# A three-stage block kernel: opening loads and weight split rearranged, pad rows written expert by expert

## The reference

```
mod = silu(c) @ wmod                     # six rows of 128 for each sequence
h = layernorm(x) * (1 + ca) + sa
x = x + ga * mamba(h)                    # 4-tap conv, selective scan with 16 states, gating
h = layernorm(x) * (1 + cb) + sb
x = x + gb * moe(h)                      # shared SwiGLU (938 wide) + top 2 of 8 SwiGLU experts
```

## Time and profile before

| what | us |
|---|---|
| median of 3 runs | 829.33 (828.41 to 831.73) |
| profiled execution | 833.42 |
| its span, first to last instruction | 831.6 |
| TensorE busy in the span | 690.9 (83%) |
| VectorE busy | 572.3 (69%) |
| ScalarE busy | 424.7 (51%) |
| GpSimd busy | 381.5 (46%) |

### The profile page before, as it was taken

One profiled execution on the slowest core, in us unless ns is written; L12 is line 12 of the kernel. 1 busy time (PEld: TensorE's weight loads), 2 busy tenths in 40 slices (PEclk: granted clock), 3 DMA queues, 4 the chain that ended last, 5 costly groups with the idle time before them and its releaser, 6 DMA issues.

```text
span 831.6 us, 11904 instructions
## 1 busy us (share of the span) xinstructions
PE 690.9 (83%) x3134; PEld 529.0 (64%) x3135; DVE 572.3 (69%) x1227; ACT 424.7 (51%) x821; POOL 381.5 (46%) x300
## 2 busy tenths in 40 slices
PE   3736889988888899887877998999989999999920
PEld 1425666756666676665645877777778777887710
DVE  3666888878788888888553665566656665666637
ACT  2413757475574757464433555555555555555510
POOL 2462264554446374555232745547228145632236
PEclk9758899999899999999787999999999999999975
DMA  7302000000000001000041203030303003000036
GB/s 236 88 1 70 20 27 25 26 25 19 6 32 19 25 26 25 26 25 27 7 162 62 95 24 108 12 108 24 98 23 94 26 16 108 25 25 27 28 108 205
DMA packets 38202, 44.37 MB, mean 53 GB/s; under 512 B 5334, under 2 KB 28880, under 8 KB 38184
## 3 DMA queue, kind: packets, MB, share of 16 engines
q1 hardware_dynamic: 33576, 35.69, 13.9%
q0 software_dynamic: 4608, 8.47, 3.1%
HBM read 31.42 MB, written 13.76 MB: 54 GB/s over the span
## 4 chain that ended last, share of the span: by engine, by line
PE 58%; DVE 22%; issue 8%; ACT 4%; DMA 2%; SPq 2%; POOL 2%; another core or an unknown queue 1%; DVEq 1%; ACTq 0%; POOLq 0%
PE PS L576 54%; PE PS L579 4%; DVE prod L1189 2%; DVE acc L1207 2%; DVE diag L1284 1%; DVE delta L1228 1%; DVE wd L1280 1%; DVE X L1308 1%; ACT L1021 1%; DVE r L1346 1%; DVE oh L1349 1%; DVE al L1194 1%; DVE stats_a L1174 1%; DVE r L1347 1%
## 5 line engine op out<-in xcount | busy, mean ns | idle before, releaser
L916 ACT ACTIVATE sg<-PS 128x512 f32<-128x512 f32 x216 | 129.3, 598 | 208.3 <-PE PS L576 179.0
L576 PE MATMUL PS<-xh,w_lo 128*128 128x512 f32 x432 | 188.6, 437 | 21.7 <-DVE prod L1189 10.5
L1189 DVE TENSOR_TENSOR PS<-PS,sg 128x512 f32<-128x512 f32 x160 | 111.9, 699 | 131.0 <-PE PS L576 111.1
L576 PE MATMUL PS<-xh,w_hi 128*128 128x512 f32 x432 | 172.8, 400 | 0.0
L576 PE MATMUL PS<-xl,w_hi 128*128 128x512 f32 x432 | 172.8, 400 | 0.0
L535 POOL DMA_INDIRECT result_dram<-y_rows,aux_d x80 | 78.0, 975 | 200.6 <-DVE y_rows L1540 161.8
L576 PEld LDWEIGHTS PS<-xh,w_lo 128*128 128x128 f32 x432 | 83.8, 194 | 52.5 <-issue 18.3
L469 POOL DMA_INDIRECT sorted_dram<-h,slot x64 | 71.3, 1115 | 93.3 <-DVE slot L1384 66.3
L1194 DVE TENSOR_TENSOR al<-PS,ah 128x512 fp32r<-128x512 f32 x160 | 109.2, 683 | 6.4 <-ACT ah L923 3.9
L923 ACT CAST ah<-PS 128x512 fp32r<-128x512 f32 x160 | 93.2, 582 | 15.2 <-DVE PS L1189 13.5
L576 PE MATMUL PS<-ah,w_lo 128*128 128x512 f32 x216 | 93.7, 434 | 4.0 <-ACT ah L923 4.0
(11 more groups left out here) (218 smaller groups left out, 1136.1 us busy)
## 6 DMA issues: line engine op xcount, KB each, us to landing
stage<-in_w_gu SPq DMA_DIRECT2D x18, 469.0 KB
xin<-sorted_dram SPq DMA_DIRECT2D x20, 260.0 KB, 2.6
stage<-in_w_dn SPq DMA_DIRECT2D x9, 448.0 KB
tab<-mods_dram SPq DMA_DIRECT2D x8, 384.0 KB, 3.5
sorted_dram<-pad SPq DMA_DIRECT2D x8, 260.0 KB
out<-X SPq DMA_DIRECT2D x4, 512.0 KB, 3.2
stage<-result_dram SPq DMA_DIRECT2D x3, 512.0 KB, 5.1
result_dram<-y_rows,aux_d POOLq DMA_INDIRECT x80
```

Of the source, the lines that this page charges most:

```text
L576: return nc.tensor.matmul(out, lhsT, rhs, start=start, stop=stop, **k)
L916: A.activation(sg[:, c % 3, :], bank("gate", where, c), ACT.Silu).then_inc(s["silu_done"], 1)
L1189: V.tensor_tensor(product_in(where, c), bank("up", where, c), sg[:, c % 3, :], ALU.mult).then_inc(s["prod_done"], 1)
```

## The change

Seven things change.

1. The three constants needed first (`mats`, `w_in`, `cols`) count on a semaphore `first_in` of their own, and only six on `consts_in`. SP no longer waits for the first chunks before it issues the next loads. `head_norm(0)` waits for no constants, `modulate(0)` only for the two modulation columns (`mods_cols`), and `project_in` no longer for `mods_rows`.
2. GpSimd clears only the three pad regions of `stage`, at the very start.
3. `head_moments` and `head_root` cover 4, 14 and 14 chunks instead of 4, 4 and 24. VectorE does the first 14 after `conv`, the other 14 after `make_delta`; GpSimd does the third root after `pairs_by_b(0)`.
4. The shared weights are split by ACT (one copy of 128x3072 to `w_hi`, after `keep_next` in `body(0)`) and VectorE (three subtractions of 128x1024, in `body(0)`).
5. GpSimd releases `split_done` 2 before `body(G-1)`, and SP loads the raw weights of x = 2 before it waits for the plan.
6. SP writes the pads of expert 0 only ahead of the first tile, and those of expert e+1 after the tile loads of expert e; the wait for `split_done` and the next raw load follow, and `tiles_of` stands behind these.
7. In the last shared expert the count matmul comes after chunk 2's gate and up, ACT does chunk c+1's silu ahead of chunk c's high part, VectorE one product ahead.

```diff
@@ sync
-            load_x(0, GC)
-            sp.wait_ge(s["x_in"], 16)
+            load_x(0, GC, "x_in")
...
-            const(mats[:].rearrange("p m t -> p (m t)"), a["big"])
+            first(mats[:].rearrange("p m t -> p (m t)"), a["big"])
...
-            load_x(GC, CH - GC)
+            load_x(GC, CH - GC, "x_more")
...
+            sp.wait_ge(s["split_done"], 2)
+            load_raw(2)
             sp.wait_ge(s["plan_ready"], 1)
             sp.wait_ge(s["setup_mem"], 2)
-            for e in range(E):
-                row = sp.value_load(plan[0:1, 2, e:e + 1], min_val=e * REGION, max_val=e * REGION + TOKENS)
-                sp.dma_start(sorted_dram[bass.ds(row, TILE)].rearrange("(p r) d -> p (r d)", p=P),
-                             pad[:].rearrange("p r d -> p (r d)")).then_inc(s["pads_out"], 16)
-            sp.wait_ge(s["pads_out"], 16 * E)
+            pad_rows(0)
             sp.wait_ge(s["sorted_out"], 16 * 2 * CH)
...
-            with sp.Fori(0, E - 1) as e:
-                expert(e, True)
-            count = expert(E - 1, False)
+            with sp.Fori(0, E - 2) as e:
+                expert(e)
+                pad_rows(e + 1)
+                sp.wait_ge(s["split_done"], e + 3)
+                load_raw(e + 3)
+            expert(E - 2)
+            pad_rows(E - 1)
+            count = expert(E - 1)
@@ gpsimd
-            pool.wait_ge(s["mods_pe"], 1)
-            V.memset(stage[:], 0.0).then_inc(s["stage_clear"], 1)
             pool.wait_ge(s["consts_in"], 16 * NCONST)
-            head_root(2, GC, GC)
             expand_c(0)
-            split_hi(0, 0)
-            head_root(3, 2 * GC, CH - 2 * GC)
+            head_root(2, GC, EARLY)
@@ tensor
-                    count_picks(G - 1, LAST_COUNTS)
                 if c == 2:
                     pe.wait_ge(s["y_out"], G - 1)
                 if c < FC:
                     gate_up(0, G - 1, c, WIDE)
+                if c == 2:
+                    count_picks(G - 1, LAST_COUNTS)
@@ scalar
+            def split_high():
+
+                act.wait_ge(s["raw_in"], 16 * NRAW)
+                A.copy(w_hi[0][:], stage[:]).then_inc(s["split_hi"], 1)
...
-            act.wait_ge(s["consts_in"], 16 * NCONST)
             head_norm(0, 1)
-            act.wait_ge(s["mods_rows"], 1)
+            act.wait_ge(s["mods_cols"], 1)
             modulate(0)
+            act.wait_ge(s["first_in"], 16 * NFIRST)
@@ vector
+            dve.wait_ge(s["x_more"], 16)
+            head_moments(GC, EARLY)
             dve.wait_ge(s["a_neg_ready"], 1)
...
             make_delta(0)
+            head_moments(GC + EARLY, CH - GC - EARLY)
             level_exponents(0)
...
             pairs_by_c(0)
-            head_moments(2 * GC, CH - 2 * GC)
```

More of the change, by code:

```diff
@@ L298, in _, with load_x, first @@
             x_view = a["x"].rearrange("(c p) d -> p c d", p=P)
[L300 to L301 removed]
+            def load_x(c0, n, done):
+                sp.dma_start(X[:, c0:c0 + n, :], x_view[:, c0:c0 + n, :]).then_inc(s[done], 16)
             def const(dst, src):
                 sp.dma_start(dst, src).then_inc(s["consts_in"], 16)
[L306 to L307 removed]
+            def first(dst, src):
+                sp.dma_start(dst, src).then_inc(s["first_in"], 16)
+            load_x(0, GC, "x_in")
             sp.dma_start(c_t[:], a["c_t"]).then_inc(s["c_in"], 16)
             sp.dma_start(stage[:, 0:6 * P], a["L0_wmod"]).then_inc(s["c_in"], 16)
[L310 to L312 removed]
+            first(mats[:].rearrange("p m t -> p (m t)"), a["big"])
+            first(w_in[:].rearrange("p m t -> p (m t)"), a["L0_attn_W_in"])
+            first(cols[:], a["cols"].rearrange("(h p) d -> p h d", p=P))
+            const(w_x[:], a["L0_attn_W_x"].rearrange("(h p) d -> p h d", p=P))
+            const(a_log[:], a["a_log"].to_broadcast([P, NS]))
             const(small[:], a["small"])
@@ L344, in _, with pad_rows @@
                 load_tab_g(g)
+            def pad_rows(e):
+                row = sp.value_load(plan[0:1, 2, bass.ds(e, 1)], min_val=0, max_val=(E - 1) * REGION + TOKENS)
+                sp.dma_start(sorted_dram[bass.ds(row, TILE)].rearrange("(p r) d -> p (r d)", p=P),
+                             pad[:].rearrange("p r d -> p (r d)")).then_inc(s["pads_out"], 16)
+            sp.wait_ge(s["split_done"], 2)
+            load_raw(2)
             sp.wait_ge(s["plan_ready"], 1)
             sp.wait_ge(s["setup_mem"], 2)
-            for e in range(E):
-                row = sp.value_load(plan[0:1, 2, e:e + 1], min_val=e * REGION, max_val=e * REGION + TOKENS)
-                sp.dma_start(sorted_dram[bass.ds(row, TILE)].rearrange("(p r) d -> p (r d)", p=P),
-                             pad[:].rearrange("p r d -> p (r d)")).then_inc(s["pads_out"], 16)
-            sp.wait_ge(s["pads_out"], 16 * E)
+            pad_rows(0)
             sp.wait_ge(s["sorted_out"], 16 * 2 * CH)
@@ L360, in load_tile, with expert @@
                     s["tile_in"], 16)
-            def expert(e, more):
+            def expert(e):
                 tiles, first = tiles_of(sp, e)
-                if more:
-                    sp.wait_ge(s["split_done"], e + 2)
-                    load_raw(e + 2)
+                sp.wait_ge(s["pads_out"], 16 * (e + 1))
+                apart(sp)
                 with sp.Fori(0, tiles) as t:
@@ L1044, in _ @@
             pair_decays(0)
-            def step(I, c, where):
-                silu(I, c, where)
-                high(I, c, where)
             def body(g, prev, head):
@@ L1064, in body @@
                 keep_next(g)
+                if not prev:
+                    split_high()
                 if prev:
@@ L1111, in _ @@
             copy_h2(G - 1)
+            silu(G - 1, 0, WIDE)
             for c in range(FC):
-                if c == 1:
+                if c + 1 < FC:
+                    silu(G - 1, c + 1, WIDE)
+                if c == 0:
                     router_exp(G - 1)
-                step(G - 1, c, WIDE)
+                high(G - 1, c, WIDE)
             keep_result(G - 1, WIDE)
@@ L1323, in second_norm, with split_low @@
                 V.engine_nop().then_inc(s["tab_free"], 1)
+            def split_low(k):
+                n = WC // 3
+                at = slice(k * n, (k + 1) * n)
+                if k == 0:
+                    dve.wait_ge(s["split_hi"], 1)
+                last = V.tensor_tensor(w_lo[0][:, at], stage[:, at], w_hi[0][:, at].bitcast(F32), ALU.subtract)
+                if k == 2:
+                    last.then_inc(s["split_done"], 1)
             def low_x(g):
@@ L1458, in body @@
                 gate_y(g, 0)
+                if not prev:
+                    split_low(0)
                 if prev:
@@ L1463, in body @@
                 gate_y(g, 1)
+                if not prev:
+                    split_low(1)
                 if prev:
@@ L1469, in body @@
                 tail_moments(g)
+                if not prev:
+                    split_low(2)
                 if prev:
@@ L1507, in _ @@
             product(g, 0, WIDE)
+            weights(g)
             low(g, 0, WIDE)
-            weights(g)
             place(g, LAST_COUNTS)
@@ L1522, in _ @@
             V.engine_nop().then_inc(s["aux_read"], 1)
+            product(g, 1, WIDE)
             for c in range(1, FC):
-                product(g, c, WIDE)
+                if c + 1 < FC:
+                    product(g, c + 1, WIDE)
                 low(g, c, WIDE)
```

33 lines of the change are left out of this document (16 added, 17 removed).

## The result

| kernel | median, us | ratio to the kernel before, 95% interval |
|---|---|---|
| before | 830.28 (828.41 to 831.73) | |
| changed | 810.09 (808.52 to 812.65) | 0.9767 (0.9734 to 0.9800) |
| changed, second comparison | 808.06, beside 829.66 | 0.9744 (0.9710 to 0.9779) |
| changed, third comparison | 808.38, beside 830.95 | 0.9757 (0.9721 to 0.9793) |

The change is worth 20.2, 21.6 and 22.6 us in the three comparisons, 21.5 on average. The profiled execution of the changed kernel took 809.22, span 807.4; that of the kernel before had taken 833.42. The pair differs by 24.2. The prediction had 24.5 for the pair and 804.8 for the median; the measured median is 810.1, inside its range of 798 to 813, with a gain 3 us smaller than forecast.

The account below looks back on a forecast made before the run. TensorE is busy 83% of the span; the prediction took its waits in the opening and at the hand-over as the losses addressed. 16.3 + 8.2 = 24.5 us off 829.3 gives 804.8, range 798 to 813.

Parts of the forecast that it names:

- First projection 4.9 ahead: Opening: modulation inputs 2 us sooner, head norm waiting for the shift alone; projection starts at 11.4, 4.9 us ahead.
- Scan factors 6.0 ahead: End of `pairs_by_c`: 4.9 + 0.8 - 1.4 - 1.3 + 3.0 from `take_dbc`, `delta`, moments' overrun and `lev_c`.
- Mixing 20.3 ahead: Opening: TensorE's matrices become the last input, 7.1 us behind `pairs_by_c`; `mix` starts at 44.5 instead of 64.81.
- 3.1 lost to ACT's copy: First gating product: ACT's 2.7 us copy delays `conv(1)`, so 6.8 us from the matrices instead of 3.7.
- 0.9 lost to the third subtraction: Between `tail_moments` and `take_dbc`: VectorE's subtraction puts softplus ahead of ACT's tail norm; 0.9 us lost (0 to 2.5).
- Loop entered 16.3 ahead: Start of the looped groups: 20.3 - 3.1 - 0.9 = 16.3 us ahead.
- Looped groups 0: Looped groups wait only on the program's own progress, so an earlier start should reach the end whole.
- Hand-over 8.2: First tile: gated result at 432.2 and tile landing at 432.3 meet; start near 432.5, 8.2 us ahead (6 to 9).
- Borders 0, tiles 0: Expert borders: tiles issued 1.2 to 1.6 us later, but slack of 0.6 or more; 0 lost (to 4).
- From the profiled execution to the median: Whole kernel: profiled execution would come to 808.9; the median, 4.1 lower, loses the same 24.5 us, to 804.8.
- first two rivals: First: split stays on the path, 812, chance 0.13. Second: expert borders starve, four at 1 to 2 us, 810, chance 0.10.
- third rival: More than forecast: `delta` is not blocked, or TensorE's clock is higher in the denser opening; 798, chance 0.09.

Follow-up runs that it names:

- e1: The changed kernel timed once more with no edit, beside the kernel before at 829.66: 808.06 us, ratio 0.9744.

## Why the prediction was right, and where its terms were off

The median of 810.1 (808.1 and 808.4 later) lies in the range of 798 to 813, and the mechanism is the forecast one. The gain itself was forecast 3 us too large, and the small gap of the profiled pair (24.2 against 24.5) is luck, as the terms show:

- **First projection 4.9 ahead.** 16.34 - 11.62 = 4.7. The inputs of the modulation came only 1.0 sooner (6.22), not 2.0; in e1 they came at 5.49 and the projection started at 11.12, 5.2 ahead. Items 1 and 2 were not run alone, so this term rests on these rows.
- **Scan factors 6.0 ahead.** GpSimd's pairs and VectorE's end as forecast: `pairs_by_c` ended at 36.4 (it started at 35.14, 1.28 long), where it had started at 41.39, so 6.3. All four pieces are in the rows: no late `take_dbc`, `delta` 1.41, the moments' overrun, `lev_c` 0.42.
- **Mixing 20.3 ahead.** It was 22.8 (64.81 - 42.04), or 21.8 over four profiles with the old opening (mean 63.94) and four with the new (42.11). The forecast took TensorE's 7.1 us from `pairs_by_c` to its matrices as a constant. They were measured at a granted clock of 0.50 (42.60 to 49.65); here it was 0.70 from 36.4 to 40 and 1.00 from 40 to 48, and TensorE needed less. The run with the moved subtractions had the same program up to mixing and a clock of 0.50 from 35.7 to 43: 43.45 - 35.13 = 8.3 from GpSimd's pairs to mixing, against 42.04 - 35.90 = 6.1.
- **3.1 lost to ACT's copy.** 22.8 ahead at mixing, 20.1 at the first gating product (67.78 - 47.70): 2.7. The copy was forecast at 2.7 and took 2.76.
- **Not forecast: 1.7 lost to the half clock.** VectorE's gating, with a subtraction between the two halves, left TensorE idle for 5.19 us, and the output products took 3.75 instead of 2.02.
- **0.9 lost to the third subtraction.** From 18.6 ahead at the end of the output products (76.19 - 57.55) to 17.8 when group 1's pairs start on GpSimd. The row `rstd_b` shows why: 1.03 us beside the subtraction, 0.24 in the run where the subtraction stood elsewhere. This is the blocking the other way round, of GpSimd by a VectorE operation, which the rows of before had not shown. By the rule on the shared ports (the Trainium skill, SBUF — State Buffer, "SBUF: two separate sides") it should happen, and the trace agrees.
- **Loop entered 16.3 ahead.** It was 17.8 to 18.9, by which engine one takes. Over four profiles with the old opening (mean 89.44) and four with the new (71.63) it is 17.8 by TensorE's first shared product, and 16.9 by GpSimd's pairs of group 1 (89.16 and 72.29). The 0.9 between the two is the router's products ahead of the loop, which took 2.2 to 2.4 us in the four old profiles and 1.66 in the new ones, as the granted clock was higher there (0.70 from 88 to 90.3 in the kernel before, 1.00 from 70 to 74 in the changed one).
- **Looped groups 0.** From the first shared product to the last `tab_g` it is 315.05 us on average in the four old ones and 316.65 in the four new. So 1.6 were given back by that mark, and 0.7 from GpSimd's pairs on: more than half of the 1.6 is the head start of TensorE alone that was just named. Two of the new ones are at 315.3 and two at 318.0, one of each on the same chip, so four profiles can hardly tell the rest from nothing; what sets a group's pace there stays open.
- **Hand-over 8.2.** The pair shows 8.2 (34.70 - 26.47 from the last `tab_g` to the first tile), but by chance, and twice. Over three profiles with the old SP order the 34.70 is 33.98, and over the nine with both items and the new order the 26.47 is 28.3. So the term is 5.7 (6.6 for the three profiles of the changed kernel alone). The step that failed is "the last down products lose waits of 2.2 and 0.4 us ... the gated result comes at 432.2 instead of 436.2": of these 4.0 us the order gives next to nothing (no gain in time alone, at most half a microsecond in the profiles), and the pause of 1.91 at 428.05, which I let it absorb, stands in no other profile.
- **Borders 0, tiles 0.** 0.17 at one border; from the first tile to the results 362.5 before, 363.1 and 361.9 and 361.8 after.
- **From the profiled execution to the median.** The prediction took the same 24.5 off the median, as if the two executions differed by a constant 4.1. But the profiled execution of before was long in just the places above: by 0.9 in its opening, 0.6 in its groups and 0.7 in its hand-over against the means just given. Part of what I counted as gain was that. The sum that the marks give is 17.8 - 1.6 + 5.7 = 21.9, and the measured one 21.5.

By the time alone the first two rivals (812 and 810) fit the 810.1 better than the 804.8; it is the rows that rule their mechanisms out. The split did not stay on the path as in the first one: ACT's copy took 2.76 and not 5.3, and `diag` 0.69. Part of its conditions held, though: a low clock behind the opening, and a blocked operation at the third subtraction. The borders did not starve. Of the third rival one condition held, the higher clock ahead of mixing, and it was worth some 2 us there (6.1 against 8.3); the half clock at the output products took 1.7 back.

## What to carry to other kernels

A queue's order counts by what stands between the last event and the transfer that is waited for: moving four issues out of there gave nearly all of the hand-over's gain, while seven pads less gave next to nothing. Before an operation is moved to another engine, list which operations of the neighbour it will run beside, and not only those that were slow before; a wait taken from one pair can come back at the next. And a profiled pair that agrees to 0.3 us with the forecast proves little when single executions of one kernel differ by 4: set each term against several profiles, and by the marks of more than one engine. A clock that comes back in one stretch can be lost in the next: look at the granted clock up to the mark that is compared.

## What the runs showed of the hardware

- VectorE and GpSimd block each other both ways: `dl_upto` 5.29 instead of 0.22 beside a GpSimd operation of 5.30; `rstd_b` on GpSimd 1.03 instead of 0.24 beside a subtraction of 1.22; `c_exp` 2.94 instead of 1.96.
- The same 16 output products took 3.75 at a granted clock of 0.50 behind 5.19 us of idle, 2.46 behind 2.62, 2.02 behind 1.59 (the kernel before) and 1.95 behind none.
- In one comparison the executions of the changed kernel differ with their mean granted clock: 804.5 and 804.9 at 0.929, 808.2 at 0.923 and 813.0 at 0.913. It isn't so everywhere: of the hand-over-only kernel the fastest execution (821.2) had 0.910 and the slowest (826.3) 0.914. One chip of the three ran the kernel before at 0.907 in the median and 832.5 us, the others at 0.913 and 0.914, 829.7 and 831.0 us.
